# A two-layer graph kernel on Trainium2: the prologue and the edge stage in one program block, with the first loads, gathers and edge units in another order

## The reference, cut to what matters

```python
h = jnp.maximum(_layernorm(x, axis=-1), 0.0)
edge_feat = jnp.concatenate([h[src], h[dst], edge_attr], axis=-1)
m = mish(edge_feat @ W1 + b1)
messages = mish(m @ W2 + b2)
agg = jax.ops.segment_sum(messages, dst, num_segments=1250)
...
u = mish(jnp.concatenate([h, agg], axis=-1) @ W3 + b3)
x = x + layernorm_affine(h + u @ W4 + b4)
# then a second layer: relu of a low-rank product, gathered and summed over the same edges
```

## Time and profile before

| | us |
|---|---|
| median of three runs | 1574.95 (1574.72 to 1576.31) |
| the profiled execution | 1574.38 |
| its span, first to last instruction | 1572.7 |
| first table matmul | 16.5 |
| first B table matmul | 58.0 |
| first message matmul | 127.2 |

### The profile page before, as it was taken

The page is one execution under the profiler, slowest core; times in us unless marked ns, Lnnn a source line. Parts: engine busy times, 40 slices in busy tenths (PEclk is TensorE's granted clock), DMA queues, the critical chain, the costliest instruction groups (busy, mean ns, idle before and its releaser), DMA issues.

```text
span 1572.7 us, 33395 instructions
## 1 busy us (share of the span) xinstructions
PE 1502.9 (96%) x7862; PEld 1171.4 (74%) x7862; DVE 1418.9 (90%) x2916; ACT 1296.9 (82%) x2503; POOL 1078.2 (69%) x984
## 2 busy tenths in 40 slices
PE   4948999999999999999999999999999999999998
PEld 3736777777777777777777777777777777776785
DVE  5647999999999999999999999999999999996666
ACT  3117999999999999999999999999999999996462
POOL 1215787888787787878778877878878888763220
PEclk9968999999999999999999999999999999999999
DMA  7663454544554544554555545445544555455563
GB/s 248 222 235 103 117 125 115 127 118 113 121 121 116 128 115 117 125 122 114 122 120 120 123 114 127 118 118 126 122 114 121 122 119 124 114 139 126 134 138 153
DMA packets 122435, 205.09 MB, mean 130 GB/s; under 512 B 31625, under 2 KB 54281, under 8 KB 122400
## 3 DMA queue, kind: packets, MB, share of 16 engines
q0 software_dynamic: 59392, 116.85, 33.8%
q1 hardware_dynamic: 60896, 85.21, 17.6%
q10 hardware_dynamic: 2112, 2.62, 0.5%
HBM read 151.60 MB, written 42.75 MB: 124 GB/s over the span
## 4 chain that ended last, share of the span: by engine, by line
PE 88%; DVE 3%; issue 1%; DMA 1%; ACT 1%; SPq 0%; DVEq 0%; POOLq 0%; ACTq 0%
PE bm L1003 55%; PE bp L988 7%; PE bp L990 6%; PE bs L1026 5%; PE bp L992 5%; PE pm L1014 2%; PE po L1932 2%; PE pm L1013 1%; PE pu L1910 1%; PE pu L333 1%; PE pu L1977 1%; DMA M<-M 1%; PE pu L1964 0%; DVE x L2204 0%; PE pt L1946 0%
## 5 line engine op out<-in xcount | busy, mean ns | idle before, releaser
L911 POOL TENSOR_TENSOR hTl<-tp,hTh 128x512 fp32r<-128x512 f32 (+1 forms) x316 | 414.2, 1311 | 228.8 <-DVE khl L1184 212.6
L1003 PE MATMUL bm<-W2h,hTh 128*128 128x512 f32 x1252 | 497.4, 397 | 0.5 <-DVE bm L1177 0.5
L1003 PE MATMUL bm<-W2l,hTh 128*128 128x512 f32 x1252 | 496.5, 397 | 0.0
L1003 PE MATMUL bm<-W2h,hTl 128*128 128x512 f32 x1252 | 494.7, 395 | 0.0
L900 POOL DMA_INDIRECT xg<-A_tab,idx x309 | 324.1, 1049 | 56.7 <-issue 47.8
L1057 ACT ACTIVATE rp<-bp 128x512 f32<-128x512 f32 (+1 forms) x316 | 184.9, 585 | 140.2 <-PE bp L992 139.0
L1003 PEld LDWEIGHTS bm<-W2h,hTh 128*128 128x128 f32 x1252 | 235.3, 188 | 69.0 <-DVE bm L1177 14.3
L1003 PEld LDWEIGHTS bm<-W2l,hTh 128*128 128x128 f32 x1252 | 235.3, 188 | 57.5
L1003 PEld LDWEIGHTS bm<-W2h,hTl 128*128 128x128 f32 x1252 | 235.4, 188 | 53.4
L1149 DVE SCALAR_TENSOR_TENSOR rp<-rp 128x512 f32<-128x512 f32 (+1 forms) x316 | 217.8, 689 | 47.5 <-ACT rp L1057 35.5
L1158 DVE SCALAR_TENSOR_TENSOR tp<-rp,bp 128x512 f32<-128x512 f32 (+1 forms) x316 | 212.6, 673 | 6.0 <-ACT rp L1063 3.6
(11 more groups left out here) (223 smaller groups left out, 2347.1 us busy)
## 6 DMA issues: line engine op xcount, KB each, us to landing
ea<-in_eaT SPq DMA_DIRECT2D x156, 128.0 KB
M_tab<-mev POOLq DMA_DIRECT2D x157, 80.0 KB
agg_tab<-ev POOLq DMA_DIRECT2D x157, 64.0 KB
db<-in_dst_rows SPq DMA_DIRECT2D x78, 128.0 KB
M<-M SPq DMA_DIRECT2D x78, 128.0 KB
eaW<-Bh_tab SPq DMA_DIRECT2D x79, 64.0 KB
eaW<-Bl_tab SPq DMA_DIRECT2D x79, 64.0 KB
xg<-A_tab,idx POOLq DMA_INDIRECT x313
```

The source lines that it names most:

```text
L911: e.tensor_tensor(hTl[p][:, j, 0:w], tp[u.const % 2][:, 0:w], hTh[p][:, j, 0:w], ALU.subtract)\
L1003: last = e.matmul(bank[0:r, :], a[p][:, c, j * P:j * P + r], w[:, c, :], start=False, stop=c == KC - 1 and w is W2l, skip_group_check=True)
```

## The change

- **One block.** The prologue's programs are run at the head of each engine's program in the same block as the edge stage. The barrier and SP's wait for all stores are gone; instead each engine waits for the semaphore count of `bases` before it loads the register, and single waits stand where the edge stage needs them (`b_stored`). `bases` moves ahead of the first B store.
- **x in three loads** (two, three, five chunks), with variances and scales in three batches. W1's high and low parts are separate steps, and a table takes its twelve matmuls in the order high-high, low-high, high-low, so that it starts when `nTh` and the high part of W1 are there.
- **Loads between A's stores.** The second half of W1 is started after the first A store, W2 after the second, index columns and b1 after the fifth, and the inputs of groups 0 and 1 after the seventh and eighth. `ta` has four buffers.
- **Groups 0 and 1 are gathered in the prologue**, eight gathers in a row; POOL's `zero_m` 2 to 5 stand behind them and wait for earlier B tables. The last four `zero_m` move from ACT's queue to SP's, behind the rows of B for groups 0 and 1 and ahead of group 2's inputs.
- **A bank for each of the first four units**: `bp0`, `bp1`, `pm`, `bs`. PE does the sixteen transposes of group 0 first (`gathered`) and then the eight products (`products`); ACT takes the twelve activations of these units in the order `ORDER`. DVE prepares groups 0 and 1 and copies the bias ahead of all of it.

The core of the diff (moved code that only changes its indentation is left out):

```diff
-BATCH = [(0, 5), (5, NCH)]
+TA = 4
+BATCH = [(0, 2), (2, 5), (5, NCH)]
...
+        prologue.of[engine](e)
+        known(e)
         span = e.value_load(wide_i[0:1, 0:1], min_val=0, max_val=NP)
...
-                    i = c % 2
-                    e.wait_ge(c_A, c + 1)
-                    if c >= 2:
-                        e.wait_ge(q_sa[i], 16 * (c // 2))
-                    e.activation(ta[i][:], pA[i][:, :], ACT.Copy).then_inc(c_ta, 1)
+                i = c % TA
+                e.wait_ge(c_A, c + 1)
+                if c >= TA:
+                    e.wait_ge(q_sa[i], 16 * (c // TA))
+                e.activation(ta[i][:], pA[c % 2][:, :], ACT.Copy).then_inc(c_ta, 1)
...
-                    between = {1: [lambda: variances(1)], 2: [windows], 3: [lambda: scales(1), iotas],
-                               5: [lambda: split_w1(1)], 6: [w2_hi], 7: [w2_lo], 8: [columns]}
+                between = {0: [lambda: variances(1), lambda: scales(1)], 1: [lambda: variances(2)], 2: [windows],
+                           3: [lambda: scales(2), iotas], 4: [lambda: w1_hi(1)], 5: [lambda: w1_lo(1)], 6: [w2_hi],
+                           7: [w2_lo], 8: [columns], 9: [bases]}
...
-                    store_b(e, 0)
-                    bases()
-                    for c in range(1, NCH):
-                        store_b(e, c)
+                for c in range(NCH):
+                    store_b(e, c)
...
-                    e.wait_ge(q_ix[0], 16)
-                    for i in range(2):
-                        e.wait_ge(q_sa[i], 16 * (NCH // 2))
-                    for t in range(SUB):
-                        e.indirect_dma_start(out=xg[0][:, t, :].bitcast(F32), out_offset=None, in_=A_d,
-                                             in_offset=bass.IndirectOffsetOnAxis(ap=idx[0][:, t:t + 1], axis=0))\
-                         .then_inc(q_ga[0], 16)
-                    for i in range(2, M_EARLY):
-                        e.wait_ge(c_B, 2 * i)
-                        zero_m(e, i, q_z)
+                a_stored(e)
+                for g in range(2):
+                    e.wait_ge(q_ix[g], 16)
+                    for t in range(SUB):
+                        e.indirect_dma_start(out=xg[g][:, t, :].bitcast(F32), out_offset=None, in_=A_d,
+                                             in_offset=bass.IndirectOffsetOnAxis(ap=idx[g][:, t:t + 1], axis=0))\
+                         .then_inc(q_ga[g], 16)
+                for i in range(2, M_EARLY):
+                    e.wait_ge(c_B, i + 2)
...
-                            c0, c1 = BATCH[i]
+                        if c == (0, 2, 4)[i]:
...
-                        if c == 0:
-                            e.wait_ge(c_v.sem, v["w1", half])
-                        for k in range(KC):
-                            for a, w in ((nTh, w1h), (nTl, w1h), (nTh, w1l)):
-                                last = e.matmul(bank[:, :], a[:, k, c * P:(c + 1) * P], w[:, half * KC + k, :],
+                    for a, w, part in ((nTh, w1h, "w1h"), (nTl, w1h, None), (nTh, w1l, "w1l")):
+                        if part and c == 0:
+                            e.wait_ge(c_v.sem, v[part, half])
+                        if half == 0 and a is nTl:
+                            e.wait_ge(c_lo, c + 1)
+                        for k in range(KC):
+                            last = e.matmul(bank[:, :], a[:, k, c * P:(c + 1) * P], w[:, half * KC + k, :],
+                                            start=n == 0, stop=n == 3 * KC - 1)
...
-                        e.wait_ge(c_lo, c + 1)
+                    e.wait_ge(c_hi, c + 1)
...
-                    e.dma_start(xs[:, 0:half, :], xv[:, 0:half, :]).then_inc(q_x[0], 16)
-                    w1_half(0)
-                    e.dma_start(xs[:, half:NCH - 1, :], xv[:, half:NCH - 1, :]).then_inc(q_x[1], 16)
+                for i, (c0, c1) in enumerate(BATCH):
+                    c1 = min(c1, NCH - 1)
+                    e.dma_start(xs[:, c0:c1, :], xv[:, c0:c1, :]).then_inc(q_x[i], 16)
+                    if i == 0:
+                        w1_half(0)
...
-                    w1_half(1)
-                    for a, b in HALF:
-                        e.dma_start(wcraw[a:b, :], W1[2 * H:2 * H + ED, :]).then_inc(q_w2, 16)
-                    e.dma_start(W2raw[:], W2.rearrange("(c p) n -> p c n", p=P)).then_inc(q_w2, 16)
-                    e.dma_start(scoli[:], src_cols).then_inc(q_col, 16)
-                    e.dma_start(wcol[:], ew_cols).then_inc(q_col, 16)
-                    e.dma_start(b1b[:], row_bcast(b1, H, P)).then_inc(q_b1, 16)
-                    e.dma_start(b2b[:], row_bcast(b2, H, P)).then_inc(q_b2, 16)
+                for c in range(NCH):
+                    e.wait_ge(c_ta, c + 1)
+                    e.dma_start(A_d[c * P:(c + 1) * P, :], ta[c % TA][:]).then_inc(q_sa[c % TA], 16)
+                    if c == 0:
+                        w1_half(1)
+                    if c == 1:
+                        for a, b in HALF:
+                            e.dma_start(wcraw[a:b, :], W1[2 * H:2 * H + ED, :]).then_inc(q_w2, 16)
+                        e.dma_start(W2raw[:], W2.rearrange("(c p) n -> p c n", p=P)).then_inc(q_w2, 16)
+                    if c == 3:
+                        e.wait_ge(c_v.sem, v["win"])
+                        e.dma_start(win_d, win[:]).then_inc(q_win, 16)
+                    if c == 4:
+                        e.dma_start(scoli[:], src_cols).then_inc(q_col, 16)
+                        e.dma_start(wcol[:], ew_cols).then_inc(q_col, 16)
+                        e.dma_start(b1b[:], row_bcast(b1, H, P)).then_inc(q_b1, 16)
+                    if c == 5:
+                        e.wait_ge(q_win, 16)
+                        e.dma_start(base_b[:].rearrange("p g a -> p (g a)"),
+                                    row_bcast(win_d.rearrange("g a -> (g a)"), 4 * NG, P)).then_inc(q_winb, 16)
+                        e.dma_start(b2b[:], row_bcast(b2, H, P)).then_inc(q_b2, 16)
+                    if c in (6, 7):
+                        first_inputs(c - 6)
...
+        ORDER = [(0, 0), (1, 0), (0, 2), (2, 0), (0, 3), (1, 2), (3, 0), (1, 3), (2, 2), (2, 3), (3, 2), (3, 3)]
...
+            e.wait_ge(s_prep, 1)
+            copy(0, G)
+            e.wait_ge(s_prep, 3)
+            copy(1, G)
+            b_stored(e)
+            rows(0, b[0])
+            rows(1, b[1])
+            for i, n in zip(range(M_EARLY, NCH), (1, 2, 2, 3)):
+                e.wait_ge(s_pre, n)
+                zero_m(e, i, q_zlate)
+            with e.Fori(1, FULL // 2) as i:
...
+            for j in range(SUB):
+                gathered(At(None, j))
+            for j in range(SUB):
+                products(At(None, j))
+            slots(e, SUB - PRE_AHEAD, LOOP0, LOOP1, LAST, step)
...
+            for j, k in ORDER:
+                pre_chain(At(None, j), k)
+            slots(e, SUB - PRE_AHEAD, LOOP0, LOOP1, LAST, step)
...
+            for g in range(2):
+                for k in range(3):
+                    prep(At(None, g * SUB), k)
+            e.wait_ge(q_b2, 16)
+            e.wait_ge(c_ta, NCH)
+            for j in range(SUB):
+                e.tensor_copy(bm[j][:, :], b2b[:]).then_inc(v_bias, 1)
+            adjacency(At(None, 0))
+            u = [At(None, j) for j in range(SUB + 1)]
+            square(u[0])
+            square(u[1])
+            square(u[2])
+            pre(u[0], 0)
+            pre(u[0], 1)
+            square(u[3])
+            for j in range(1, SUB):
+                pre(u[j], 0)
+                pre(u[j], 1)
+            square(u[4])
+            prep(At(None, 2 * SUB), 0)
+            slots(e, 0, LOOP0, LOOP1, LAST, step)
...
```

598 lines of the change are left out of this document (301 added, 297 removed).

## The result

The changed kernel takes 1549.46 us in the median of four runs (1545.88 to 1550.23), the kernel before in the same session 1575.63 (1574.72 to 1578.33): a ratio of 0.983, 95% interval 0.981 to 0.985. The forecast was 1547, its range 1541 to 1556. The profiled execution took 1548.88 us, its span went from 1572.7 to 1547.2, 25.5 us less (26.2 in the medians); predicted were 27.8.

What follows compares the result with a forecast made beforehand. PE was taken to bound the edge stage, so only the start could shrink: 1.7 + 8.0 + 0 + 8.9 + 9.2 = 27.8 us off 1574.4 gives 1546.6, forecast as 1547 for the median; range 1541 to 1556.

Steps and rivals of the forecast that it cites:

- Wrong would be: Signs against the forecast: PE waiting for chunk 2 or nTl; B tables over 34 us; unit 3's low part late; longer edge stage.
- A side (first B table): Start and A tables together: the first B table comes 9.7 us sooner, at 48.3 and not 58.0.
- B tables to T: The ten B tables up to DVE's last split: 0 gain, bounds 2.8 us shorter and 8 us longer.
- passage: From DVE's last split to the first edge product: 7.3 us and not 16.2, a gain of 8.9.
- first units (product to slot 1): The first four edge units, first product to first message: 9.8 us and not 19.0, a gain of 9.2.
- 1.7 for x in three loads: At the start: chunk 3's transposes at 22.9 us instead of 24.64, from smaller loads and tables from high parts first.
- ta and loads: In the A tables: four ta buffers and loads between A's stores remove ACT's 8.3 us wait; PE gains 8.0 us.
- The rival in which ACT still waits: In the A tables: ACT still waits for A's first store; 1555 us, chance 0.02.
- zeros 2.8 us apart: In the B tables: the 640 KB zero fills come 2.8 us apart instead of 5.6, counted against the change.
- B's stores are crowded: Rival, B tables: gathers and closer zeros delay store landings, 3 to 8 us longer; 1550 to 1555 us, chance 0.17.
- zeros ahead of group 2: Rival, first units: group 2's inputs land late, first messages held up 3 to 5 us; 1550 to 1552, chance 0.12.
- The clock as the case that decides against the change: Rival, A and B tables: short pauses keep PE at the lower clock, 2.5 us more per table; 1597 us, chance 0.02.

Runs made afterwards that it cites:

- x_two: The changed kernel with x in two loads and statistics in groups of five and five chunks: 1550.65 us, ratio 0.985.
- front_two: The changed kernel with all loads ahead of A's stores again and two ta buffers, x still in three loads: 1557.94 us, ratio 0.990.
- loads_front: The changed kernel with all loads ahead of A's stores again, ta keeping four buffers: 1549.02 us, ratio 0.984.
- zeros_paced: The changed kernel with POOL's M_tab fills 2 to 5 at every second step of the B tables, as before: 1546.97 us, ratio 0.983.
- four_tb: The changed kernel with four buffers for B's splits, the wait for the store moved from the sum to the split: 1542.21 us, ratio 0.978.
- drained: The changed kernel with every engine waiting for all A and B stores to land before the edge stage: 1549.56 us, ratio 0.984.
- zeros_act: The changed kernel with the four late M_tab fills on ACT's queue right behind B's last split, not on SP's: 1552.44 us, ratio 0.986.
- zeros_behind: The changed kernel with the four late M_tab fills behind group 2's loads on SP's queue, not ahead: 1551.40 us, ratio 0.984.

## Why the prediction was right, and where its sizes were off

The waits that the prediction named are the ones that the change takes away, and the time fell where it was forecast. The sum is partly right by luck: its terms are off by 1.8, 2.5, 0.3 and 2.7 us, 7.3 in all, and as two of these errors raise the gain and two lower it, 3.1 are left. All four signs under "Wrong would be" came: PE waits 2.05 us for chunk 2 and 0.90 for nTl; the B tables take 34.6 us; unit 3's low part starts 3.8 us behind unit 2's; and from the first message to the end it takes 1449.0 us, where it took 1445.5. At slot 1, predicted gains beside measured ones:

| step | predicted | measured |
|---|---|---|
| A side (first B table) | 9.7 | 11.5 |
| B tables to T | 0 | -2.5 |
| passage | 8.9 | 9.2 |
| first units (product to slot 1) | 9.2 | 6.5 |
| sum | 27.8 | 24.7 |

The other 0.8 us of the 25.5 lie behind slot 1, well inside the scatter of that stretch.

*Start.* Of 1.7 for x in three loads the trace shows 4.7 at chunk 3. The term was built from a point that came nearly as predicted, the second scale at 16.3 (15.65 measured). Behind it I put 6.6 us up to chunk 3's transposes, where 4.3 are seen: 0.9 to chunk 2's at 16.56, then one chunk of 3.37. I had taken the slow pace of the first chunks of before for that of the second chunk. The term stood for the third load and the order of the matmuls together; x_two gives the load 1.9 of the 4.7 at this point, and 3.8 at the first B table.

*ta and loads.* Predicted 8.0, seen 6.8 (33.3 us from chunk 3 to the first B table before, 26.5 after). The 1.15 us that are missing are one chunk's 4.37 instead of 3.22, the wait for nTl: the third batch of five statistics, which I had fitted in "with over 1 us left", stands right where chunk 2's low part is due. The rival in which ACT still waits is out; front_two shows what it would have been, and that two edits guard against it. In loads_front, with the loads in front, the longest A store takes 11.8 us and four buffers leave 4.9 of wait; after's takes 8.4. The Trainium skill (DMA: Bandwidth & Descriptors, "Queues, rings and completion order") says that a DMA engine takes the descriptors of one ring, here the transfers that SP starts, in order. These traces agree: the stores that stand behind the loads land late.

*B tables.* The step that failed is "zeros 2.8 us apart". That is the spacing of their waits on PE's progress. By the time that POOL had waited 12.9 us for A's stores and issued eight gathers, at 62.0, PE was through tables 4 and 5, and it was through table 6 at 63.2: two of these waits had been met, the third was met at once, and three fills went out in 2.45 us. Of the 3.2 us by which the tables take longer than before 1.7 are waits of PE for DVE (4.2 in sum, 2.5 before) and about 1.6 the lower clock behind the longest of them. This is the rival "B's stores are crowded" in its mechanism, just under its lower end (3 to 8 us), and zeros_paced and four_tb confirm it from both sides.

*Passage.* T+6.95 against T+7.3, close, but by errors that cancel. I had the rows of B wait for the last store until T+4.3. That store landed 2.3 us after its issue at 83.36, not 3.9, so at T+2.7. The rows were issued at T+4.57 all the same, since SP was not ready: between its last store and the first copy it loads three registers (`wide_i` at 83.9 us, `base_i` at 85.0 and 85.5), which the sum doesn't have, so the copies M<-M start at T+3.1 and not T+1.5, and the rows stand behind them. Then the rows were quicker, 0.5 us to issue and 1.9 to land, not 0.7 and 2.3. Whether the rows ahead of the copies would gain anything no run shows. Where the 9.2 us come from, drained and zeros_act show in part: 2.2 the wait for the stores, 5.3 the fills beside the transfers, if they add up and if fills that start 5.3 us earlier cost as much as before's; some 1.7 are left for the barrier and for the copies that are now prepared earlier, which no run tried alone. In zeros_act the last Bl store, issued at 83.08 behind ACT's first fill (82.76), lands at 86.6, ahead of that fill (4.6 us from issue to landing, at 87.3). That fits what the same section of the Trainium skill says, that a DMA engine changes round between rings. But beside the fills SP's transfers are slower: this store takes 3.6 us and not 2.3, and the first product comes 4.0 us after the issue of Bl's rows and not 1.9.

*First units.* The first message came 8.3 us after the first product, where I had it begin at 9.3 and counted 9.8 with a wait of 0.5 in it, and so sooner than forecast (98.20 for 99.4). Then 4.2 us are given back up to slot 1, of which I had 0.5: that PE runs without a gap from the first message on, so that every microsecond there counts in full, did not hold. 2.3 are the wait for unit 3's low part: the gather of group 2 began at T0+10.8 where I had its indices at T0+9.7, and PE, with its message begun at T0+7.0 and not 8.0, asked a microsecond sooner. Of the other 1.9 the clock has 1.3: slot 1 takes 5.2 us for 3.9, with the granted clock at 0.72 between 105 and 111 us. Here the rival "zeros ahead of group 2" was right in mechanism: zeros_behind finds 3.7 us in it. In the forecast it had 3 to 5 us at a chance of 0.12.

The clock as the case that decides against the change did not come: the A tables run at 1.00 from 20 to 40 us. In small it came twice, each time behind an idle stretch of PE: 1.6 us in the B tables (0.57 from 74 to 78 us), and the 1.3 us of slot 1 behind the passage (0.61 from 80 to 100 us).

## What to carry to other kernels

Where two edits guard one wait (more buffers, fewer transfers in front), undo both together before pricing either; one at a time both look cheap here (2.3 and 1.4 us, and 10.1 together). Transfers that are paced by another engine's progress can go out in a burst once their own engine has been held up, so look at what stands ahead of them, not at the spacing of their waits. A buffer for each transfer in flight took stores of 5.8 us off the path, where pacing the transfers only moved the wait; and read a change of the start at a milestone of the start, since the end scatters by more than its parts. And check a forecast by its terms and its signs of being wrong: here the time came out while all four signs had come.

## What the runs showed that I had not expected

- A store of 256 KB took 7.1 us to land in the median while the transfers moved 346 GB/s, against 2.0, and it cost nothing with four buffers.
- Issuing itself gets longer in traffic: SP's Bl_tab store takes 0.43 us to issue in most places and 1.25 at 65.32 us, its B row load 0.35 after and 1.79 in zeros_act. What is behind it on SP waits as well.
- An edge stage that started 3.7 us earlier did not end earlier (zeros_behind): from slot 1 to the end it took 1444 us, 7 more than after's 1437. The 5.4 us wait for a gather and the 2.6 us of lower clock in the slot behind it are as large as that.
